# Last stage of a graph network on Trainium2: one-hots by ScalarE in place of VectorE

## The chip, the cores and the metric

The kernel runs on one core of a Trainium2 chip. The metric is the device time in microseconds, the median of several executions. Engines are called TensorE (PE; its weight loads are PEld), VectorE (DVE), ScalarE (ACT), GpSimd (POOL) and SyncE (SP, which here only starts DMAs). They run side by side and wait for each other on semaphores.

## What is computed

Two layers of a graph network on 3125 nodes of 512 features, with 50000 edges sorted by their target. The first layer is an attention over the edges, the second a mean over neighbours with two matrices. Cut to what matters, with `deg` the number of edges into a node, at least 1:

```python
h = maximum(layernorm(x), 0)
q, k = h @ Wq + bq, h @ Wk + bk                       # 8 heads
attn = softmax over the edges of a target of (q[rows] . k[cols])
x = x + segment_sum(attn * k[cols], rows) @ Wo + bo
h2 = maximum(layernorm(x), 0)
agg = segment_sum(h2[src], dst)                       # the last stage from here
x = x + h2 @ W1.T + b1 + (agg / deg) @ W2.T + b2
```

## The kernel before, in words

**Tiling.** The nodes are cut into NW = 25 windows of WIN = 125. The sorted edges are cut into chunks of 128 x CT = 128 x 17 edges, each belonging to one window, with padding; for these inputs the last stage has 25 chunks. `key` words hold the edge's source and target; chunk tables tell where each chunk begins, which window it belongs to and whether it continues one.

**Stages.** (1) layernorm, q and k, sorting of edges, up to about 400 us. (2) attention, chunk by chunk, to about 1205 us. (3) the Wo stage, about 1205 to 1323 us: for each window t, TensorE transposes the attention's rows (`wo_cols`) and multiplies by Wo (`wo`, L769 through `product`), VectorE adds the residual and takes statistics (`wo_sum`, `wo_stats`, `wo_norm`, L1396 to L1420), ScalarE takes the square root (L697) and makes h2 by a Relu (L700) in `h2`, and GpSimd's queue stores h2 to DRAM (`store_h2`, L540). ScalarE runs this by `ahead(act, NW, 2, h2_turned, h2)`: the copy of columns for window t+2 (`h2_turned`, with L567), then `h2` for window t. VectorE's L1412 of window t also waits until the store of window t-2 has landed. (4) the last stage, to the end.

**The last stage.** For chunk g, with b = g mod 2 for its buffers:
- GpSimd gathers 17 tiles of 128 rows of h2 by an indirect DMA each (L504), into `rows[:, b]`.
- VectorE in `agg(g)`: waits for TensorE's sum, adds it to `acc` (L1439), divides by the degree (L1445, `win_out`), then runs `next_hot`: it decodes chunk g+2 (L1216 to L1223: `idx` for the gathers and `loc`, the position of each edge's target in the window), makes the one-hots `oh` of chunk g+2 (`one_hot`, L1232) and sums them over the 17 tiles (`sum_hot`, L1387, for the degrees). Only after that it adds bias (L1456) and residual (L1459) to chunk g's product, which frees the store.
- TensorE in `agg(g)`: waits for `kept` (the sum of one-hots of chunk g), 34 matmuls one-hot x rows (L929), the product of the window's own h2 with W1 (L769), transposes of `win_out` and, when SyncE's load has landed, of the rows of h2 of chunk g+1 (`fin_cols`, L915), then the product with W2 (L769).
- ScalarE in `fin(g)`: two copies of transposed columns out of PSUM (`fin_turned`, L716), the second of them for the rows of chunk g+1. Nothing else in this stage.
- SyncE in `aggregate(g)`, in this order: the loads of indices and parameters of chunk g+2 (L367, L368), the load of h2 rows of chunk g+1 (`load_rows`, L449), the store of chunk g's output (`store_out`, L456); it waits until this store has landed before it goes on.

So the loads of the next round stand behind the store of this one on SyncE's queue, and the store stands behind VectorE's work for chunk g+2. Sets of one-hots 0 and 1 are made by VectorE after its Wo loop, before `agg(0)`:

```python
            for b in range(2):
                sum_hot(b, b)
```

`ag["oh_ready"]` counts finished sets of one-hots, `ag["acc_ready"]` finished sums of TensorE, `ag["decode"]` three steps for each decoded chunk. `within(g, count)` is true without a branch for g below 25.

Of the kernel before, what the change touches and what calls it, by code (L numbers as in the profile page):

```python
# [10 lines left out]
def build(nc, io):  # L11
# [5 lines left out]
    ALU, ACT, AX = mybir.AluOpType, mybir.ActivationFunctionType, mybir.AxisListType  # L17
# [5 lines left out]
    WIN = 125  # L23
    NW = N // WIN
# [3 lines left out]
    CT = 17  # L28
# [20 lines left out]
    with ctx:  # L49
        def sb(name, shape, dt=F32):  # L50
            return ctx.enter_context(nc.sbuf_tensor(name, shape, dt))
# [43 lines left out]
        oh = sb("oh", [128, 2, CT, WIN])  # L95
# [16 lines left out]
        oh_sum = junk[:, 0, 0:2 * WIN].rearrange("p (b n) -> p b n", b=2)  # L112
# [4 lines left out]
        bias = (acc, win_out)  # L117
# [28 lines left out]
        loc = sb("loc", [128, 2, CT + 2])  # L146
# [11 lines left out]
        ones = sb("ones", [128, 128])  # L158
        iota_i = arena[:, 4 * COLS:4 * COLS + 128].bitcast(I32)
        iota = sb("iota", [128, 128])  # L160
# [13 lines left out]
        whole_turn = turn[1][0:H, 0:256].rearrange("p (k n) -> p k n", k=2)  # L174
        alphap = turn[1][0:WIN, 256:256 + H]
        aggp = sums[0:WIN, 0:D]
        degp = tiny[0:WIN, 0:1]
        totp = tiny[:, 0:2 * NW].rearrange("p (j w) -> p j w", j=2)
        turned_keys = [sums[:, 0:COLS], sums[:, COLS:2 * COLS]]
# [2 lines left out]
        bias_parts = sem("bias_parts")  # L182
        XG = 5
        XT = NW // XG
        COUNTED = 20
        ROW_SPLIT = [(0, 112), (112, WIN)]
        x_in, w_in, bias_in, ends_in = [sem(f"x_in{n}") for n in range(XG)], sem("w_in"), sem("bias_in"), sem("ends_in")
# [35 lines left out]
        def chunk_sems(p):  # L223
            s = {n: sem(f"{p}_{n}") for n in ("pk_free", "idx_ready", "decode", "oh_ready", "step",
                                              "acc_free", "acc_ready", "out_ready", "out_free")}
            s["pk_in"] = [sem(f"{p}_pk_in{b}") for b in range(2)]
            s["rows_in"] = [[sem(f"{p}_rows_in{b}_{n}") for n in range(len(PARTS))] for b in range(2)]
            s["rows_free"] = [sem(f"{p}_rows_free{n}") for n in range(len(PARTS))]
            last = "store" if p == "at" else "kept"
            s[last] = sem(f"{p}_{last}")  # L230
            return s

        at, ag = chunk_sems("at"), chunk_sems("ag")
# [24 lines left out]
        def pairs(eng, n, body):  # L258

            for t in range(n):  # L260
                body(t, t % 2, t // 2)

        def ahead(eng, n, depth, first, body):

            for d in range(depth):
                first(d, d % 2, d // 2)

            def both(t, b, i):
                first(t + depth, (b + depth) % 2, i + (b + depth) // 2)
                body(t, b, i)  # L270
            pairs(eng, n - depth, both)
            for t in range(n - depth, n):
                body(t, t % 2, t // 2)

        def given(eng, condition, body):

            if condition is True:
                body()
            elif condition is not False:
                with eng.If(condition):  # L280
                    body()

        def within(g, count):
            return True if isinstance(g, int) and g < NW else g < count

        def rounds(eng, bound, pair):

            for i in range(SURE + 1):
                pair(i)
            with eng.If(bound > 2 * SURE + 2):  # L290
                with eng.Fori(0, GMAX // 2 - SURE - 1) as k:
                    pair(k + (SURE + 1))

        def chunks(eng, count, body):

            def pair(i):
                for b in range(2):
                    given(eng, within(i * 2 + b, count), lambda: body(i * 2 + b, b, i))
            rounds(eng, count, pair)
# [13 lines left out]
        def chunk_count(eng, j):  # L313
            return eng.value_load(chunk_i[0:1, j, 2, LAG:LAG + 1], min_val=NW, max_val=GMAX - 1)

        def chunk_count_after(eng, j):
            eng.wait_ge(sort_ready, j + 1)
            return chunk_count(eng, j)
# [5 lines left out]
        def _(sp):  # L324
# [5 lines left out]
            def load_x_group(n):  # L330
                tab = io["x"].rearrange("(t p) d -> p t d", p=WIN)[:, n * XT:(n + 1) * XT, :]
                for p0, p1 in ROW_SPLIT:
                    sp.dma_start(x_sb[p0:p1, n * XT:(n + 1) * XT, :], tab[p0:p1, :, :]).then_inc(x_in[n], 16)
            load_x_group(0)
# [218 lines left out]
        def _(act):  # L553
            def norm(n):

                group = rstd[:, n * XT:(n + 1) * XT]
                act.wait_ge(var_ready, n + 1)
                act.activation(group, group, ACT.Sqrt).then_inc(std_ready, 1)
                act.wait_ge(norm_ready, n + 1)
# [5 lines left out]
            def turned(t, b, i, s, ring, n=1):  # L565
                act.wait_ge(s["turn_ready"], t + 1)
                act.activation(ncol[:, b, :, :], turn[b][:, 0:KC * WIN].rearrange("p (c n) -> p c n", c=KC), ACT.Copy).then_inc(s["col_ready"], 1)  # L567
                act.wait_ge(s["col_ready"], t + 1)
                act.sem_inc(s["turn_free"], 1)
# [6 lines left out]
            def count_sides(k):  # L576

                for _ in range(k):
                    n = next(counts)
                    if n >= SIDES:  # L580
                        act.wait_ge(side_done, n - SIDES + 1)
                    act.activation(sides[:, n % SIDES, :], endf[:, n // NW, :], ACT.Sign, bias=edge[0:EP, n % NW:n % NW + 1],  # L582
                                   accum_out=cnt[:, n // NW, n % NW:n % NW + 1]).then_inc(side_done, 1)

            act.wait_ge(endf_ready, 1)
            count_sides(COUNTED)

# [20 lines left out]
            for t in range(NW):  # L608
                if (t + 4) % XT == 0 and t + 4 < NW:
                    norm((t + 4) // XT)  # L610
                if t + 1 < NW:
# [7 lines left out]
                act.activation(k_stage[t % STAGES], wide[t % 2][0:WIN, D:2 * D], ACT.Copy)  # L619
                if t < (2 * NW - COUNTED) // 3:  # L620
                    count_sides(3)
# [81 lines left out]
            def h2_turned(t, b, i):  # L703
# [1 line left out]
                act.activation(spare[:, :], ones[0:1, 0:1], ACT.Sqrt).then_inc(table_in, 1)  # L705
                act.wait_ge(table_in, t + 1)
                turned(t, b, i, s3, 2)
            ahead(act, NW, 2, h2_turned, h2)

            count1 = chunk_count_after(act, 1)  # L710

            def fin_turned(k, n, free):

                act.wait_ge(s5["turn_ready"], n)
                act.sem_inc(free, 1)
                act.activation(ncol[:, k, :, :], turn[k][:, 0:KC * WIN].rearrange("p (c n) -> p c n", c=KC), ACT.Copy).then_inc(s5["col_ready"], 1)  # L716
# [3 lines left out]
            def fin(g, b, i):  # L720
                fin_turned(1, g * 2 + 2, ag["out_free"])
                fin_turned(0, g * 2 + 3, s5["row_free"])
            chunks(act, count1, fin)


        @block.tensor
        def _(pe):
# [21 lines left out]
            def totals():  # L749
                pe.wait_ge(side_done, 2 * NW)  # L750
                pe.matmul(totp, ones[0:EP, :], cnt[:, :, :], start=True, stop=True).then_inc(tot_ready, 1)
# [32 lines left out]
            def leave(t, part, left):  # L784

                pe.wait_ge(part_ready[part], t + 1)
                pe.matmul(wide[t % 2][0:WIN, 0:D], minus[:, :], part_stage[t % STAGES][:, part, :], start=False, stop=True, skip_group_check=True).then_inc(left, 1)  # L787
# [3 lines left out]
            for t in range(NW):  # L791
# [13 lines left out]
                if t > 0:  # L805
                    leave(t - 1, 1, tail_left)
                if t == (2 * NW - COUNTED) // 3 + 1:
                    totals()
# [139 lines left out]
        def _(dve):  # L948
# [8 lines left out]
            def moments(n):  # L957

                dve.wait_ge(x_in[n], 16 * len(ROW_SPLIT))
                for t in range(n * XT, (n + 1) * XT):  # L960
                    dve.bn_stats(stats[:, t, :], x_sb[:, t, :]).then_inc(s1["step"], 1)
# [269 lines left out]
            def one_hot(s, g, b):  # L1231
                dve.tensor_tensor(oh[:, b, :, :], iota[:, 0:WIN].unsqueeze(1).to_broadcast([128, CT, WIN]),  # L1232
                                  loc[:, b, 1:CT + 1].unsqueeze(2).to_broadcast([128, CT, WIN]), ALU.is_equal).then_inc(s["oh_ready"], 1)
# [147 lines left out]
            count1 = chunk_count(dve, 1)  # L1381

            def sum_hot(g, b):

                one_hot(ag, g, b)
                dve.wait_ge(ag["oh_ready"], g + 1)
                dve.tensor_reduce(oh_sum[:, b, :], oh[:, b, :, :].rearrange("p t n -> p n t"), AX.X, ALU.add).then_inc(ag["kept"], 1)  # L1387
            for b in range(2):
                decode(ag, b, b, 0)

# [37 lines left out]
            for b in range(2):  # L1428
                sum_hot(b, b)
# [54 lines left out]
```

## Time and profile before

| | |
|---|---|
| median of 3 executions | 1931.77 us (1930.68 to 1932.28) |
| the profiled execution: time / span | 1932.3 us / 1930.5 us |
| TensorE matmuls / loads busy | 1666.8 us (86%) / 963.8 us (50%) |
| VectorE busy | 1336.3 us (69%) |
| ScalarE busy | 1001.1 us (52%) |
| GpSimd busy | 1141.1 us (59%) |
| gathers of the last stage, L504 | 425, mean 1049 ns |
| one-hots by VectorE, L1232 | 25, mean 2373 ns |
| their sums, L1387 | 25, mean 4165 ns |

Busy times are shares of the whole span, over stages with different limits. The span is what lies between the first and the last recorded instruction; the time of an execution has some us more around it. A row of a view names the line, the engine, the operation, output<-input, and in brackets the idle time before it with what ended it.

### The profile page before, as it was taken

How to read it: one execution, taken by the hardware profiler on the slowest of the kernel's cores; microseconds unless marked ns; L12 is line 12 of the kernel's file. 1: busy time of each engine (PE TensorE's matmuls, PEld its weight loads, DVE VectorE, ACT ScalarE, POOL GpSimd, SP SyncE). 2: the span in 40 equal slices, each digit the busy share in tenths (PEclk: the TensorE clock that was granted, in tenths of full speed). 3: DMA queues.
4: the chain of work that ended last, by engine and by line, in shares of the span. 5: the costliest groups of instructions: out<-in, count | busy, mean ns of one | idle time of the engine just before them, and what ended most of it. 6: DMA issues, size and time to landing. Idle time of an engine off the chain costs nothing.

```text
span 1930.5 us, 24219 instructions
## 1 busy us (share of the span) xinstructions
PE 1666.8 (86%) x5735; PEld 963.8 (50%) x5735; DVE 1336.3 (69%) x2587; ACT 1001.1 (52%) x3779; POOL 1141.1 (59%) x1323
## 2 busy tenths in 40 slices
PE   3799863688988889898888897895999999999998
PEld 1344331466666666666666666342444444444443
DVE  8768994888888989898988885465444444444441
ACT  4453313499999999999999997241000000000000
POOL 2000001878787878888787880013777777777773
PEclk9899876799999989999999999997999999999999
DMA  8122104665657565665657562945777777777774
GB/s 188 52 69 71 63 28 145 192 168 143 192 150 190 160 184 170 168 186 163 191 149 197 145 179 61 222 109 153 210 217 212 219 218 219 216 214 211 215 213 140
DMA packets 133201, 318.07 MB, mean 165 GB/s; under 512 B 41908, under 2 KB 42158, under 8 KB 133044
## 3 DMA queue, kind: packets, MB, share of 16 engines
q0 software_dynamic: 70240, 229.93, 41.8%
q1 hardware_dynamic: 62804, 86.44, 16.2%
q8 instruction: 50, 0.82, 0.2%
q14 instruction: 107, 0.88, 0.1%
HBM read 280.43 MB, written 35.86 MB: 164 GB/s over the span
## 4 chain that ended last, share of the span: by engine, by line
PE 51%; DVE 20%; issue 15%; POOL 7%; DMA 4%; ACT 2%; DVEq 1%; SPq 0%; POOLq 0%; ACTq 0%
PE wide L769 14%; PE sums L929 12%; PE sums L832 12%; PE wide L860 9%; POOL arena L504 7%; DVE nodes L1338 2%; DVE arena L1083 2%; DVE arena L1082 2%; DMA h2tab<-node 2%; DVE nodes L1284 1%; DVE nodes L1329 1%; DVE node L1225 1%; PE wide L782 1%; PE wide L787 1%; ACT arena L582 1%
## 5 line engine op out<-in xcount | busy, mean ns | idle before, releaser
L636 ACT ACTIVATE nodes<-arena,nodes 128x64 f32<-128x64 f32 x2840 | 682.7, 332 | 1.2 <-PE sums L832 1.2
L504 POOL DMA_INDIRECT arena<-ktab,idx x425 | 421.5, 992 | 188.1 <-issue 142.2
L504 POOL DMA_INDIRECT arena<-h2tab,idx x425 | 445.7, 1049 | 135.8 <-issue 134.9
L832 PE MATMUL sums<-nodes,oh 128*125 128x260 f32 x1768 | 466.7, 407 | 47.0 <-DVE nodes L1284 47.0
L769 PE MATMUL wide<-w_sb,node 128*125 128x512 f32 x1000 | 465.6, 610 | 20.7 <-ACT node L567 12.3
L832 PEld LDWEIGHTS sums<-nodes,oh 128*125 128x125 f32 x1768 | 342.0, 198 | 123.3 <-DVE nodes L1284 58.4
L929 PE MATMUL sums<-arena,oh 128*125 128x512 f32 x850 | 375.9, 600 | 6.9 <-DMA arena<-h2tab,idx 6.5
L716 ACT ACTIVATE node<-wide 128x500 f32<-128x500 f32 x51 | 27.3, 585 | 570.9 <-PE wide L915 570.8
L860 PE MATMUL wide<-q_win,node 125*128 125x512 bf16 x1275 | 310.3, 381 | 3.0 <-issue 3.0
L769 PEld LDWEIGHTS wide<-w_sb,node 128*125 128x125 f32 x1000 | 187.0, 193 | 230.8 <-issue 201.8
L1329 DVE TENSOR_TENSOR nodes<-wide,arena 128x1024 f32<-128x1024 f32 (+1 forms) x225 | 258.6, 1159 | 12.4 <-PE wide L860 11.8
L929 PEld LDWEIGHTS sums<-arena,oh 128*125 128x125 f32 x850 | 158.1, 189 | 204.7 <-issue 188.2
L1338 DVE TENSOR_REDUCE nodes<-nodes 128x16 f32<-128x1024 f32 (+1 forms) x225 | 256.9, 1151 | 0.0
L528 POOL TENSOR_SCALAR oh<-iota,loc 128x125 f32<-128x125 f32 x425 | 245.6, 592 | 0.8
L1439 DVE SCALAR_TENSOR_TENSOR acc<-acc,first_chunk,sums 125x512 f32<-125x512 f32 x25 | 18.7, 748 | 305.4 <-PE sums L929 305.4
L860 PEld LDWEIGHTS wide<-q_win,node 125*128 125x128 bf16 x1275 | 178.4, 141 | 91.9 <-issue 5.9
L510 POOL DMA_DIRECT2D sorted_tab<-arena x2 | 1.2, 612 | 287.8 <-DVE arena L1129 287.8
L1083 DVE TENSOR_TENSOR arena<-arena 128x256 f32<-128x256 f32 x272 | 113.9, 419 | 0.0
L1082 DVE TENSOR_TENSOR arena<-arena 128x256 f32<-128x256 f32 x272 | 113.6, 418 | 0.0
L1387 DVE TENSOR_REDUCE junk<-oh 128x125 f32<-128x2125 f32 x25 | 104.1, 4165 | 0.9
L540 POOL DMA_DIRECT2D h2tab<-node x25 | 13.4, 535 | 150.3 <-ACT node L700 144.4
L1232 DVE TENSOR_TENSOR oh<-iota,loc 128x2125 f32<-128x2125 f32 x25 | 59.3, 2373 | 4.0 <-DVE loc L1223 4.0
(202 smaller groups left out, 1165.9 us busy)
## 6 DMA issues: line engine op xcount, KB each, us to landing
node<-node_tab SPq DMA_DIRECT2D x27, 531.2 KB
q_win<-qtab SPq DMA_DIRECT2D x26, 336.0 KB
arena<-ktab,idx POOLq DMA_INDIRECT x425, 5.1
arena<-h2tab,idx POOLq DMA_INDIRECT x425, 3.9
h2tab<-node POOLq DMA_DIRECT2D x25, 250.0 KB, 2.7
node<-h2tab SPq DMA_DIRECT2D x26, 224.0 KB
qtab<-q_win SPq DMA_DIRECT2D x17, 336.0 KB
nodes<-x SPq DMA_DIRECT2D x5, 1120.0 KB
```

Of the source, the lines that this page charges most:

```text
L504: gp.indirect_dma_start(rows[:, b, t, :], None, tab, bass.IndirectOffsetOnAxis(ap=idx[:, b, t:t + 1], axis=0)).then_inc(s["rows_in"][b][PA ...
L528: last = gp.tensor_scalar(oh[:, b, t, :], iota[:, 0:WIN], loc[:, b, t + 1:t + 2], None, ALU.is_equal)
L636: last = act.activation(msgs[:, t, h // HH, h % HH * DH:(h % HH + 1) * DH], rows[:, 1 - b, t, h * DH:(h + 1) * DH], ACT.Copy, scale=den_in ...
L769: last = pe.matmul(out, ncol[:, b, c, :], w_sb[:, w, c, :], start=start and c == 0, stop=stop and c == KC - 1)
L832: last = pe.matmul(halves[:, u, :], oh[:, 1 - b, t, :], rhs[side][:, t, u, :], start=t == 0, stop=t == CT - 1)
L860: last = pe.matmul(wide[n % 2][:, (t - t0) * D:(t - t0 + 1) * D], ohT[:, b, :].rearrange("p (e t) -> p t e", t=CT)[:, t, :], q_win[:, b, p ...
L929: last = pe.matmul(aggp, oh[:, b, t, :], rows[:, b, t, :], start=t == 0, stop=t == CT - 1)
L1082: self.made(dve.tensor_tensor(new[:, :, 0, :], old[:, :, 0, :], old[:, :, 1, :], ALU.min))
L1083: self.made(dve.tensor_tensor(new[:, :, 1, :], old[:, :, 0, :], old[:, :, 1, :], ALU.max))
L1329: made.append(st.mark(dve.tensor_tensor(prod[:, n % 3, 0:k * D], wide[n % 2][:, 0:k * D], rows[:, b, t0:t0 + k, :].rearrange("p t d -> p ( ...
L1338: summed.append(st.mark(dve.tensor_reduce(sc[:, :, t0:t0 + k].rearrange("p h t -> p t h"), prod[:, (n - 1) % 3, 0:k * D].rearrange("p (t h ...
L1387: dve.tensor_reduce(oh_sum[:, b, :], oh[:, b, :, :].rearrange("p t n -> p n t"), AX.X, ALU.add).then_inc(ag["kept"], 1)
```

## The change

Each set of one-hots of the last stage is made by ScalarE in two steps: 17 activations, one for a tile, `(loc - iota)^2` for 125 columns, with `loc` as a per-partition bias; then one activation over all 2125 columns, `relu(1 - v)`, which gives 1 where the square was 0 and 0 elsewhere. Set g+2 is made in `fin(g)` behind the two copies. Sets 0 and 1 are made in the Wo stage, behind `h2` of windows 4 and 8. `oh_ready` counts two steps for a set. VectorE's `sum_hot` waits for the set and keeps the sum. `late_oh` is another name for `oh`.

```diff
+        late_oh = oh
+        HOT_AT = {4: 0, 8: 1}
@@ ScalarE
-            ahead(act, NW, 2, h2_turned, h2)
+            def late_hot(g, b, done=None):
+                act.wait_ge(ag["decode"], g * 3 + 3)
+                if done is not None:
+                    act.wait_ge(ag["acc_ready"], done)
+                for t in range(CT):
+                    last = act.activation(late_oh[:, b, t, :], iota[:, 0:WIN], ACT.Square, bias=loc[:, b, t + 1:t + 2], scale=-1.0)
+                last.then_inc(ag["oh_ready"], 1)
+                act.wait_ge(ag["oh_ready"], g * 2 + 1)
+                hot = late_oh[:, b, :, :].rearrange("p t n -> p (t n)")
+                act.activation(hot, hot, ACT.Relu, bias=ones[:, 0:1], scale=-1.0).then_inc(ag["oh_ready"], 1)
+
+            def h2_and_hot(t, b, i):
+                h2(t, b, i)
+                if t in HOT_AT:
+                    late_hot(HOT_AT[t], HOT_AT[t])
+            ahead(act, NW, 2, h2_turned, h2_and_hot)
@@ fin(g, b, i), ScalarE
                 fin_turned(1, g * 2 + 2, ag["out_free"])
                 fin_turned(0, g * 2 + 3, s5["row_free"])
+                given(act, within(g + 2, count1), lambda: late_hot(g + 2, b, g + 1))
@@ sum_hot(g, b), VectorE
-                one_hot(ag, g, b)
-                dve.wait_ge(ag["oh_ready"], g + 1)
-                dve.tensor_reduce(oh_sum[:, b, :], oh[:, b, :, :].rearrange("p t n -> p n t"), AX.X, ALU.add).then_inc(ag["kept"], 1)
+                dve.wait_ge(ag["oh_ready"], g * 2 + 2)
+                dve.tensor_reduce(oh_sum[:, b, :], late_oh[:, b, :, :].rearrange("p t n -> p n t"), AX.X, ALU.add).then_inc(ag["kept"], 1)
```

## Rows read from the trace of the kernel before

**Rows 1.** Busy time by stretch: us, busy and count per engine, PEclk, DMA share, GB/s.

```profile
1460.00:1900.00 440.00, 433.33 (x1139) 197.62 (x1138) 188.37 (x242) 20.35 (x38) 341.01 (x326) 1.00 0.74 216
```

**Rows 2.** Chain of waits, last stage: start us, us, what.

```profile
1583.34 4.68 DMA arena<-h2tab,idx
...
1615.75 3.43 PE wide L769 x8
...
1638.88 3.43 PE wide L769 x8
```

**Rows 3.** Timeline of one chunk: start us, us, engine, line; two SyncE rows are another chunk's.

```profile
1604.62 1.24 SPq L456 DMA_DIRECT2D out<-node  x2
1611.56 0.90 SPq L449 DMA_DIRECT2D node<-h2tab  x2
...
1619.01 2.37 DVE L1232 TENSOR_TENSOR oh<-iota,loc 128x2125 f32<-128x2125 f32 x1 [0.17 <-DVE loc L1223]
1619.34 0.46 PEld L915 LDWEIGHTS wide<-ident,node 125*128 125x128 f32 x4
1619.73 1.06 ACT L716 ACTIVATE node<-wide 128x500 f32<-128x500 f32 x2 [22.07 <-PE wide L915]
1621.41 4.16 DVE L1387 TENSOR_REDUCE junk<-oh 128x125 f32<-128x2125 f32 x1
1627.34 0.91 SPq L456 DMA_DIRECT2D out<-node  x2
1633.88 0.90 SPq L449 DMA_DIRECT2D node<-h2tab  x2
1642.48 0.46 PEld L915 LDWEIGHTS wide<-ident,node 125*128 125x128 f32 x4
```

**Rows 4.** GpSimd's timeline in the same chunk, and a row of the waits, 1325:1930.

```profile
1619.71 2.49 POOL L504 DMA_INDIRECT arena<-h2tab,idx  x1 [0.30 <-issue]
1622.50 0.95 POOL L504 DMA_INDIRECT arena<-h2tab,idx  x1 [0.30 <-issue]
...
PEld sums L929 <- DMA arena<-h2tab,idx: 16.3, 17, 4.3
```

**Rows 5.** Groups of ScalarE by shape: count, busy us, mean ns, idle before.

```profile
L636 ACT ACTIVATE nodes<-arena,nodes 128x64 f32<-128x64 f32 x2840 | 682.7, 332 | 1.2 <-PE sums L832 1.2
L582 ACT ACTIVATE arena<-junk,edge 125x400 bf16<-125x400 f32 x50 | 30.7, 619 | 9.9 <-DVEq L986 9.9
L700 ACT ACTIVATE node<-nodes,shift,rstd 125x512 f32<-125x512 f32 x25 | 20.3, 814 | 10.7 <-DVE shift L1420 10.7
L705 ACT ACT_TABLE_LOAD x1 | 1.3, 1283 | 0.7 <-issue 0.7
```

**Rows 6.** Timeline, start of last stage; median landing of gathers from the DMA view.

```profile
1330.29 0.90 SPq L449 DMA_DIRECT2D node<-h2tab  x2
1333.30 1.07 PE L915 MATMUL wide<-ident,node 125*128 125x125 f32 x4 [14.55 <-DMA node<-h2tab]
...
arena<-h2tab,idx POOLq DMA_INDIRECT x355, 4.0
```

**Rows 7.** Timeline of the Wo stage: ScalarE at windows 4, 5 and 8, VectorE at window 6.

```profile
1242.12 0.81 ACT L700 ACTIVATE node<-nodes,shift,rstd 125x512 f32<-125x512 f32 x1 [0.43 <-DVE shift L1420]
1245.92 0.20 ACT L697 ACTIVATE rstd<-rstd 125x1 f32<-125x1 f32 x1 [2.27 <-DVEq L1414]
...
1252.08 0.15 DVE L1412 TENSOR_SCALAR rstd<-mv 125x1 f32<-125x1 f32 x1 [2.96 <-POOLq L544]
...
1263.67 0.81 ACT L700 ACTIVATE node<-nodes,shift,rstd 125x512 f32<-125x512 f32 x1 [0.43 <-DVE shift L1420]
1264.61 0.59 ACT L567 ACTIVATE node<-wide 128x500 f32<-128x500 f32 x1
```

**Rows 8.** Chain of waits, Wo stage.

```profile
1265.25 3.70 PE wide L769 x8
1268.95 0.43 PE wide L764 x4
```

**Rows 9.** TensorE's timeline in the Wo stage, after a wait.

```profile
1233.05 5.37 PE L769 MATMUL wide<-w_sb,node 128*125 128x512 f32 x8 [3.17 <-ACT node L567]
```

## The prediction

> **What bounds the kernel now.** I read the page first for the stages, then the last stage by four views: busy time by stretch, the chain of waits, the timeline of one chunk, and the waits. From 1331 us to the end the kernel repeats one pattern 25 times, once for each chunk. In 440 us of it TensorE is busy for 433 at the full granted clock, ScalarE for 20, VectorE for 188 [rows 1]. The chain of waits gives the period: the products at L769 start at 1615.75 and again at 1638.88, so 23.13 us a chunk [rows 2]. TensorE waits for nobody inside it except some 0.3 us for ScalarE's copy. So the last stage is bound by TensorE, and work taken off VectorE buys nothing by itself. The chain did run through GpSimd's gathers up to 1583 us [rows 2], so GpSimd is the near second; yet TensorE's waits for gathers in the whole last stage are 16.3 us in 17 pieces, the longest 4.3 [rows 4].
>
> What is to be seen in the timeline of one chunk [rows 3] is a second loop that today has slack. P is the moment at which TensorE begins to transpose the next chunk's rows of h2 (PEld L915 node, 1619.34, next 1642.48). From P, ScalarE copies the columns (L716, over at 1620.79). VectorE has decoded chunk g+2 by then, compares (L1232, from 1619.01), sums the one-hots (L1387, from 1621.41), and only then adds the bias to chunk g's product and the residual (L1456, L1459). SyncE stores that at 1627.34 and, once the store has landed, issues the load of the next rows (L449) at 1633.88. Such a load took 3.0 us where TensorE waited for it (issued 1330.29, transposes from 1333.30 [rows 6]), so the rows are there at about 1637, some 5 us before TensorE wants them at 1642.48.
>
> **Removed.** One comparison of 128x2125 by VectorE per chunk, 2.37 us [rows 3]. While it runs, one gather's work on GpSimd lasts 2.49 us in place of 0.95 [rows 4]: 1.54 us of GpSimd per chunk. With 0.30 us between them, 16 plain gathers and this one make 16 x 1.25 + 2.79 = 22.8 us, under TensorE's 23.13, so I book the relief at nothing; its other bound is rival (b).
> The Trainium skill (SBUF — State Buffer, SBUF: two separate sides) says that a VectorE operation with two SBUF inputs and a GpSimd operation that reads SBUF shut each other out of a shared port for the whole instruction. The stretched row agrees with it. Taken as a reason for the change it would give 1.54 us a chunk wherever GpSimd is the bound, which is (b) below.
>
> **Added: the price on ScalarE.** The trace has no Square of 125 columns and no pass of 2125, so neighbours bound both. A 128x64 Copy with a per-partition scale lasts 332 ns, and 2840 of them are 682.7 us busy, so they follow each other at 0.240 us; a 400-column Sign with a per-partition bias lasts 619 ns [rows 5]. The slope between them is 287/336 = 0.85 ns a column. The 512-column Relu with both scale and bias from memory, 814 ns, gives 1.08 as upper end [rows 5]. A Square is then 0.240 + 61 x 0.00085 = 0.292 us after the one before and 0.384 us long, so 17 of them take 16 x 0.292 + 0.384 = 5.06 us (up to 5.3). The rectified pass takes 0.332 + 2061 x 0.00085 = 2.09 us (up to 2.55). With 0.1 us for the hand-overs, an estimate, a set of one-hots costs 7.25 us of ScalarE. I take the lower slope because these passes have one operand from memory, like the Sign. Square may want a table load of its own beside Sqrt: 0 or 1.28 us each way [rows 5]; I take 0 and keep the other end (5 us in all, in the Wo stage).
> The Trainium skill (ScalarE: Activation LUTs, Rules for kernel authors) advises VectorE and not ScalarE for relu, add and multiply. That speaks against this change, and the rows agree with 7.25 against 2.37 us; taken alone it says nothing of who waits, and ScalarE's idle time would make it worth 0 by [rows 1].
>
> **Where the 7.25 us lie in the last stage.** ScalarE is idle 22 of 23 us, so they fit its time. But they begin only behind its second copy, at P + 1.45, and VectorE now waits for them ahead of L1387, with the former chunk's L1456 and L1459 queued behind that wait, SyncE's store behind those, and SyncE's loads behind the store. The slack loop becomes, from P to the next P: copy 1.45 (1620.79 - 1619.34) + Squares 5.06 + rectified pass 2.09 + hand-overs 0.10 + from the start of the sum to the store's issue 5.93 (1621.41 to 1627.34) + from there to the issue of the row load 6.54 (1627.34 to 1633.88; the store's landing and two loads for chunk g+3) = 21.17 [rows 3, 5]. Then the rows must land. Bounds: 3.0 us [rows 6], and 4.0 us, the median of a gather of about the same size among all others [rows 6]. I take 3.3, nearer to the low end, because GpSimd, with 21.3 us of gathers in a longer period, will be idle about then. Sum: 24.47 us, 1.34 more than 23.13. TensorE waits that long at the transposes in each step that follows a set of one-hots. Sets are made for chunks 2 to 24, so in 23 steps; the last of these issues no load of indices ahead of its rows, which is worth about the 1.3 us, so 22 count: 22 x 1.34 = 29.5 us. Bounds: with landing 3.0 the loop is 24.17 and the stage pays 23 us; with landing 4.0, a store part of 6.94 (1604.62 to 1611.56, [rows 3]) and ScalarE's upper prices it is 26.3 and the stage pays 69, which wants all of them together.
> The delay holds the load of indices for the next decode too, but that is issued ahead of the rows, and today's decode is over at 1619.01, before P [rows 3], so it is not what comes last. The gathers hang on the decode as well; GpSimd runs half a chunk behind it, and that covers them.
>
> **Two sets in the stage before.** Sets 0 and 1 are now made by ScalarE behind windows 4 and 8 of the Wo stage. VectorE made them behind that stage, where TensorE stood 14.55 us waiting for the first rows of h2 [rows 6], hence at no cost: nothing is won at the end. ScalarE, though, is in the loop of each window. Behind window 4 (Relu over at 1242.93) its next statistics step moves from 1245.92 to 1242.93 + 7.25 + 0.8 for the copy between = 1251.0 [rows 7]. VectorE's pass takes about 3.3 us from there to L1412 of window 6, which comes at 1254.3 in place of 1252.08; it had stood there 2.96 us for a store [rows 7]. Some 2.1 us of delay stay, and I carry them to window 8; bounds 0 and 5, since the next stores are issued later too. Behind window 8 there is no cover: the copy at 1264.61 is what TensorE's products at 1265.25 wait for, and from there its products follow each other in the chain to the stage's end [rows 7, 8]. This set costs its full 7.25, with the carry 9.4 us. TensorE stands idle some 7 us before. A wait of 3.17 us at 1233.05 was followed by eight matmuls in 5.37 us against 3.70 [rows 8, 9], 1.67 lost; I add 2.0 (bounds 0 and 3.5). Stage: +11.4 us, bounds 7 and 16.
>
> **Sum.** 29.5 + 11.4 = +40.9 us on the profiled execution's 1932.3 us (span 1930.5 and 1.8 around it) = 1973.2. The profiled execution stood 0.5 us above the median of the runs, 1931.8, so the forecast is 1973 us.
>
> **Rivals.** (a) The loop stays below 23.13: it needs 1.34 us less than I count, for instance a landing and a store part shortened by a quieter DMA. Against: both store parts in the rows are over 6.5 us and the 3.0 us landing was a quiet one. Then only the Wo stage pays: 1932 + 11 = 1943 us.
> (b) Faster than before: GpSimd is the true bound of the last stage's first half, as the chain up to 1583 us has it [rows 2], and the comparison robs it of 1.54 us a chunk [rows 4]. Eleven chunks by 1.54 = 17 us off: 1915 us, if the new loop stays short and the Wo stage absorbs its sets. It decides only where TensorE's period is set by GpSimd's; against it stand GpSimd's own 22.8 us, and the 16.3 us of waits for gathers, 17 at most if all went.
> (c) ScalarE is dearer: the Squares don't overlap (0.384 apart, +1.5 us a set), or cost as the 814 ns row has it. 22 x 1.5 + 3 = 36 us more, 2009 us. Against it: 2840 passes in a row do overlap [rows 5].
> (d) The change does not bite: the sets are ready before VectorE asks for them and the windows' stores cover the rest. The queue allows it nowhere in the last stage. About 1932 us.
>
> **How the numbers follow.** Forecast 0.80; (a) 0.08; (b) 0.03; (c) 0.07; (d) 0.02. The range runs from 1950, half-way from the forecast's lower bound (23 + 7 us, 1962) to (a), to 1998, where landing is 4.0 us and the store part 6.94 (loop 25.57, +54 us, Wo stage 12). A measurement of this kernel can tell about 0.2% (4 us) from no change. Faster by more: (b), 0.03. Within: (d), 0.02. Slower: the rest, 0.95.
>
> **What would show it.** In the profile after: a period of the last stage of 24 to 25.6 us, and TensorE idle 1 to 2.4 us a chunk ahead of PE L915 node, put down to the DMA of the rows; ScalarE's set 7.0 to 7.6 us; VectorE's sum starting 8.7 us after P; no stretched gather on GpSimd, and idle time of its own; in the Wo stage the products of 1265.25 some 9 us later, and slow at first. I am wrong if the period stays 23.1, if TensorE waits for gathers or for the sum of one-hots instead, or if the Wo stage grows by less than 7 us.

## The result, and the profile after

The changed kernel takes 1994.01 us, the median of 4 runs (1990.80 to 1996.57), against 1932.03 us (1930.68 to 1933.87) for the kernel before: a ratio of 1.0319 [1.0301, 1.0337]. The forecast was 1973 us with a range of 1950 to 1998. The profiled execution took 1990.8 us, with a span of 1989.0. It is set against the former one's 1932.3.

The difference lies in two stages. I measured each between two marks that both kernels have. From the first transposes of `win_out` to the last (24 periods) the last stage went from 1363.20 to 1919.75, 556.55 us, and now goes from 1370.51 to 1978.26, 607.75 us: +51.2. Before, all periods lay between 23.13 and 23.55 us; now they range from 23.13 to 29.81 with a mean of 25.3. From the first Relu of the Wo stage to the last it was 1220.30 to 1322.44, 102.14 us, and is 1215.97 to 1330.15, 114.18 us: +12.0. The attention part, which the change doesn't touch, ended 4.3 us earlier in this execution. 1932.3 - 4.3 + 12.0 + 51.2 = 1991.2, against 1990.8.

First the page after, section 1 and two groups of section 5 (busy us, mean ns, idle before).

```profile
PE 1674.7 (84%) x5735; PEld 964.5 (48%) x5735; DVE 1276.5 (64%) x2562; ACT 1177.8 (59%) x4229; POOL 1101.6 (55%) x1323
...
L506 POOL DMA_INDIRECT arena<-h2tab,idx x425 | 405.7, 955 | 211.9 <-issue 129.2
...
L1405 DVE TENSOR_REDUCE junk<-oh 128x125 f32<-128x2125 f32 x25 | 104.1, 4167 | 219.7 <-ACT oh L720 219.7
```

VectorE and GpSimd have less to do (60 us and 40 us less), and the gathers' mean fell from 1049 to 955 ns, so the change does relieve both. What to read is the last number of the last line: VectorE now stands 219.7 us in front of its sums, waiting for ScalarE.

The stretch that answers [rows 1] (us; busy and count of PE, PEld, DVE, ACT, POOL; PEclk; DMA share; GB/s), and rows of the waits of the last stage (sum, count, longest).

```profile
1380.00:1980.00 600.00, 554.18 (x1422) 252.68 (x1421) 178.80 (x279) 181.39 (x444) 374.39 (x392) 0.97 0.68 193
...
DVE junk L1405 <- ACT oh L720: 219.7, 23, 11.2
POOL arena L506 <- DVE idx L1235: 82.7, 22, 5.9
PE wide L934 <- DMA node<-h2tab: 59.5, 22, 14.7
```

TensorE was busy 98% of such a stretch and is now busy 92%. It waits for the rows of h2, 59.5 us in all, of which 14.7 are the old wait ahead of the stage. That leaves 44.8 us in 21 steps, 2.1 each. GpSimd, the former near second, idles 82.7 us.

The chain of waits in the last stage, which answers [rows 2] (start, us, what):

```profile
1652.64 0.66 PE wide L934 x4
1653.89 5.03 ACT oh L716 x17
1658.94 2.08 ACT oh L720
...
1667.50 3.82 DMA out<-node
...
1674.61 4.26 DMA node<-h2tab
1678.91 1.09 PE wide L934 x4
```

The chain names the new loop: transposes, ScalarE's set, VectorE, store, load, transposes. From 1652.64 to 1678.91 it took 26.27 us. TensorE's products, which were the chain in [rows 2], are out of it. The timeline of the same chunk, to be laid beside [rows 3]:

```profile
1652.64 0.65 PE L934 MATMUL wide<-ident,node 125*128 125x125 f32 x4 [1.89 <-DMA node<-h2tab]
...
1653.89 5.02 ACT L716 ACTIVATE oh<-iota,loc 128x125 f32<-128x125 f32 x17
1658.94 2.07 ACT L720 ACTIVATE oh<-oh,ones 128x2125 f32<-128x2125 f32 x1
1661.04 4.17 DVE L1405 TENSOR_REDUCE junk<-oh 128x125 f32<-128x2125 f32 x1 [9.58 <-ACT oh L720]
...
1666.97 0.91 SPq L458 DMA_DIRECT2D out<-node  x2
...
1674.07 0.90 SPq L451 DMA_DIRECT2D node<-h2tab  x2
...
1678.91 1.09 PE L934 MATMUL wide<-ident,node 125*128 125x125 f32 x4 [3.52 <-DMA node<-h2tab]
1679.80 4.80 PE L788 MATMUL wide<-w_sb,node 128*125 128x512 f32 x8
```

The loop is 8.40 us to the sum (1652.64 to 1661.04), 5.93 to the store, 7.10 to the row load and 4.84 until TensorE has the rows. Over the stage, with steps that have all of these, the store part has a mean of 6.90 us (22 steps) and the landing one of 4.20 (21 steps, 2.90 to 5.18).

In the Wo stage ScalarE's timeline answers [rows 7]:

```profile
1238.57 5.01 ACT L716 ACTIVATE oh<-iota,loc 128x125 f32<-128x125 f32 x17
1243.61 2.07 ACT L720 ACTIVATE oh<-oh,ones 128x2125 f32<-128x2125 f32 x1
1246.51 0.20 ACT L699 ACTIVATE rstd<-rstd 125x1 f32<-125x1 f32 x1
...
1262.07 5.01 ACT L716 ACTIVATE oh<-iota,loc 128x125 f32<-128x125 f32 x17
1267.12 2.07 ACT L720 ACTIVATE oh<-oh,ones 128x2125 f32<-128x2125 f32 x1
1269.31 0.59 ACT L569 ACTIVATE node<-wide 128x500 f32<-128x500 f32 x1
```

and TensorE behind that last copy answers [rows 8]:

```profile
1269.94 6.70 PE L788 MATMUL wide<-w_sb,node 128*125 128x512 f32 x8 [4.97 <-ACT node L569]
```

From its Relu at 1220.30 the kernel before needed 43.37 us to the Relu of window 8. It is now 45.38: a carry of 2.0. Then the set costs its full length, and the product behind it lasts 6.70 us in place of 3.70.

### The profile page after: what moved, and what is told of

It reads as the page before. It is cut to its first block, busy times and chain, and to the rows that moved or that the text cites. A ratio compares the mean times of both kernels' runs of the same rounds, so it can differ in the third digit from the quotient of the medians.

```text
span 1989.0 us, 24669 instructions
## 1 busy us (share of the span) xinstructions
PE 1674.7 (84%) x5735; PEld 964.5 (48%) x5735; DVE 1276.5 (64%) x2562; ACT 1177.8 (59%) x4229; POOL 1101.6 (55%) x1323
## 4 chain that ended last, share of the span: by engine, by line
PE 35%; DVE 22%; issue 17%; DMA 11%; ACT 10%; SPq 3%; DVEq 1%; POOL 1%; POOLq 0%; ACTq 0%
PE wide L788 10%; PE sums L851 10%; PE wide L879 8%; ACT oh L716 6%; DMA node<-h2tab 4%; DMA out<-node 4%; PE sums L948 2%; DVE nodes L1357 2%; ACT oh L720 2%; DVE arena L1102 2%; DVE arena L1101 2%; DMA h2tab<-node 2%; DVE nodes L1303 1%; DVE node L1244 1%; DVE nodes L1348 1%
## 5 line engine op out<-in xcount | busy, mean ns | idle before, releaser
L506 POOL DMA_INDIRECT arena<-h2tab,idx x425 | 405.7, 955 | 211.9 <-issue 129.2
L788 PE MATMUL wide<-w_sb,node 128*125 128x512 f32 x1000 | 481.9, 627 | 21.0 <-ACT node L569 19.6
L851 PE MATMUL sums<-nodes,oh 128*125 128x260 f32 x1768 | 456.2, 400 | 47.3 <-DVE nodes L1303 47.3
L851 PEld LDWEIGHTS sums<-nodes,oh 128*125 128x125 f32 x1768 | 335.4, 194 | 121.2 <-DVE nodes L1303 58.7
L788 PEld LDWEIGHTS wide<-w_sb,node 128*125 128x125 f32 x1000 | 194.0, 200 | 237.3 <-issue 213.5
L734 ACT ACTIVATE node<-wide 128x500 f32<-128x500 f32 x51 | 29.5, 587 | 458.3 <-PE wide L934 458.3
L1405 DVE TENSOR_REDUCE junk<-oh 128x125 f32<-128x2125 f32 x25 | 104.1, 4167 | 219.7 <-ACT oh L720 219.7
L716 ACT ACTIVATE oh<-iota,loc 128x125 f32<-128x125 f32 x425 | 125.5, 388 | 0.0
L1102 DVE TENSOR_TENSOR arena<-arena 128x256 f32<-128x256 f32 x272 | 116.9, 430 | 0.0
L1101 DVE TENSOR_TENSOR arena<-arena 128x256 f32<-128x256 f32 x272 | 116.6, 429 | 0.0
```

The lines of the kernel that those rows point to most:

```text
L506: gp.indirect_dma_start(rows[:, b, t, :], None, tab, bass.IndirectOffsetOnAxis(ap=idx[:, b, t:t + 1], axis=0)).then_inc(s["rows_in"][b][PA ...
L716: last = act.activation(late_oh[:, b, t, :], iota[:, 0:WIN], ACT.Square, bias=loc[:, b, t + 1:t + 2], scale=-1.0)
L788: last = pe.matmul(out, ncol[:, b, c, :], w_sb[:, w, c, :], start=start and c == 0, stop=stop and c == KC - 1)
L851: last = pe.matmul(halves[:, u, :], oh[:, 1 - b, t, :], rhs[side][:, t, u, :], start=t == 0, stop=t == CT - 1)
L1101: self.made(dve.tensor_tensor(new[:, :, 0, :], old[:, :, 0, :], old[:, :, 1, :], ALU.min))
L1102: self.made(dve.tensor_tensor(new[:, :, 1, :], old[:, :, 0, :], old[:, :, 1, :], ALU.max))
```

## The experiments

The theory: VectorE's wait for ScalarE holds back chunk g's output, and with it store and row load, so this loop, some 25.5 us long, sets the period; two sets in the Wo stage add their own delay. Two repairs follow that leave the sets on ScalarE: VectorE finishes the output before it waits for the set (output first), or SyncE loads the rows ahead of the store (rows ahead). The rivals were that ScalarE's price itself, or a transfer under contention, sets the period wherever the work stands.

The twelve runs fell under two conditions. Along with the eight labelled e1 to e7 and f8 the kernel before took 2213 to 2238 us, along with f3, f4, f6 and f7 it took 1933 to 1934 us, nearly as in the result above. I call the first the long condition. Some of the expectations put it down to the chip, but chip number 7 of the record stands for both, 1934 us with f4 and 2238 us with f8; what makes the difference is not known. What tells the theories apart is read from the four runs at 1933 to 1934 us, and the others are told behind them.

**f4: output first.** Applied to the changed kernel, VectorE decodes chunk g+2 where it did, and sums its one-hots behind L1477, which frees the store:

```diff
-                def next_hot():
-                    decode(ag, g + 2, b, i + 1)
-                    sum_hot(g + 2, b)
-                given(dve, within(g + 2, count1), next_hot)
+                given(dve, within(g + 2, count1), lambda: decode(ag, g + 2, b, i + 1))
@@ behind L1477, the addition of the residual
+                given(dve, within(g + 2, count1), lambda: sum_hot(g + 2, b))
```

> The kernel of e4_output_first again, on another chip (the chips of the e runs took 2213 to 2238 us for the kernel before in place of 1932, with other waits than those of the case's profiles). On a chip that takes 1932 us for the kernel before, theory A gives 1943 us (loop cut, period 23.13, only the Wo stage pays), theory B 1994 us. On a slow chip: 0.985 of the kernel before, as measured.

Measured: 1939.94 us, ratio 1.0033 [1.0021, 1.0046]. The 24 periods take 555.48 us, 1.1 less than before the change; the Wo stage keeps its 112.56. In TensorE's timeline two transposes of `win_out` follow each other after 23.14 us, and VectorE's waits for ScalarE in the stage fell from 219.7 to 44.5 us:

```profile
1395.15 0.59 PE L934 MATMUL wide<-ident,win_out 125*128 125x125 f32 x4
...
1418.29 0.59 PE L934 MATMUL wide<-ident,win_out 125*128 125x125 f32 x4
...
DVE junk L1405 <- ACT oh L720: 44.5, 22, 2.0
```

The loss of the last stage is gone although ScalarE does the same work at the same place. So the loss came from what stood behind VectorE's wait; ScalarE's price alone does not cause it.

**f7: both repairs.** f4, and sets 0 and 1 made by VectorE behind its Wo loop, as before:

```diff
-        HOT_AT = {4: 0, 8: 1}
+        HOT_AT = {}
@@ VectorE, behind the Wo loop
-                sum_hot(b, b)
+                sum_hot(b, b, True)
@@ sum_hot(g, b, by_dve=False)
+                if by_dve:
+                    one_hot(ag, g, b)
+                    dve.wait_ge(ag["oh_ready"], g * 2 + 1)
+                    dve.sem_inc(ag["oh_ready"], 1)
```

> The kernel of e7_before_but_act again: sets 0 and 1 by VectorE behind the Wo stage, sets 2 to 24 by ScalarE, output added before VectorE waits for a set. If the chip takes about 1932 us for the kernel before: the difference to f4 (1940) is what the two sets in the Wo stage cost. By my forecast 11.4 us: 1929 to 1932 us. If f4's 6 us over the kernel before are all of their cost: 1933 us.

Measured: 1930.13 us (1928.46 to 1933.99), ratio 0.9984 [0.9974, 0.9993]. Wo stage 102.48 us, 24 periods 555.47. Against f4 it is 9.8 us faster: the price of the two sets in the Wo stage. The other repair, f4's, is worth 54 us (1994.0 to 1939.9). In this kernel's timeline the store is out before VectorE turns to the sum:

```profile
1643.78 0.69 DVE L1475 TENSOR_TENSOR node<-wide,junk 125x512 f32<-125x512 f32 x1 [5.36 <-PE wide L788]
...
1645.64 0.91 SPq L458 DMA_DIRECT2D out<-node  x2
1647.44 4.17 DVE L1409 TENSOR_REDUCE junk<-oh 128x125 f32<-128x2125 f32 x1 [2.02 <-ACT oh L720]
```

With ScalarE's sets and no cost of their own, this kernel is 3 us (0.16%) ahead of the kernel before. The interval leaves out 1, but only just, and 0.2% was what the prediction took a measurement to be able to tell. So much, or so little, is the change worth once its two costs are mended.

**f3: rows ahead.** VectorE's order as in the changed kernel; SyncE loads rows two chunks ahead, and issues that load before the store:

```diff
+            load_rows(1, 1)
...
-                load_rows(g + 1, 1 - b)
+                given(sp, within(g + 1, count1), lambda: load_rows(g + 2, b))
```

> The kernel of e3_rows_ahead again (rows of h2 loaded two chunks ahead, before the store; all else as in the changed kernel). If the chip takes about 1932 us for the kernel before: theory A 1940 us, as f4 did, since TensorE waits no more for rows; should the rest of the loop (store, load of indices, decode, set, sum) be longer than 23.13, up to 1955. Theory B, the store of the output itself or VectorE's wait is the cost and not the rows: 1984 us or more.

Measured: 1953.6 us, ratio 1.0102 [1.0081, 1.0122]; the 24 periods take 569.95 us, 37.8 less than in the changed kernel, so the row load held most of the loss, but not all. The first periods are 23.13, later ones up to 25.34. The timeline of one of these, and a row of the waits:

```profile
1650.38 0.91 SPq L458 DMA_DIRECT2D out<-node  x2
...
1662.02 0.18 DVE L1236 TENSOR_SCALAR idx<-pk 128x17 int32<-128x17 int32 x1 [9.73 <-DMA par<-chunk_tab]
...
1675.73 0.91 SPq L458 DMA_DIRECT2D out<-node  x2
1677.83 0.65 PE L935 MATMUL wide<-ident,win_out 125*128 125x125 f32 x4 [1.99 <-DVEq L1465]
...
PEld wide L935 <- DVEq L1465: 21.2, 15, 2.8
```

VectorE waits 9.73 us for the parameters of chunk g+2, whose load stands behind the store too. From store to store it is 25.35 us by way of that load, the decode, the set and the sum. My prediction had dismissed it ("not what comes last"). That was right while the rows came later; with the rows out of the way it is the next loop.

**f6: four Squares fewer.** Sets 2 to 24 leave out tiles 0 to 3, so they are 1.18 us shorter:

```diff
-                for t in range(CT):
+                for t in ((range(4, CT)) if done is not None else range(CT)):
```

> The kernel of e6_four_less again: 13 Squares in place of 17 in each set of the last stage; tiles 0 to 3 keep what their buffer held, so the sums of the second layer are not the reference's. If the chip takes about 1932 us for the kernel before: 1.17 us less in the loop, theory A 22 x 1.17 = 26 us less, 1968 us; with TensorE's slow stretches after long waits gone as well, 1960 us or less. Theory B (ScalarE's idle time hides the set) 1990 us or more.

Measured: 1977.02 us, ratio 1.0226 [1.0206, 1.0246]; periods 590.12 us in sum, 17.6 less than with all Squares, where 22 x 1.18 = 26 us would go if nothing else in the loop moved. That lies between the two theories' times, so both missed the size; but the time did fall by 17 us, so the set does stand in the loop. What was lost is in the landing, whose mean rose from 4.20 to 4.60 us. One step, with GpSimd's gather beside the row load:

```profile
1663.96 0.95 POOL L506 DMA_INDIRECT arena<-h2tab,idx  x1 [0.30 <-issue]
1664.40 0.90 SPq L451 DMA_DIRECT2D node<-h2tab  x2
...
1669.43 0.65 PE L934 MATMUL wide<-ident,node 125*128 125x125 f32 x4 [1.24 <-DMA node<-h2tab]
```

The load is issued while a gather runs, and takes 5.03 us. Of the 22 steps in which TensorE waited for it, 17 had the load issued during the gathers or up to 0.22 us behind them, and it took 4.21 to 5.55 us; in the other 5 it was issued 0.45 to 0.67 us behind and took 3.43 to 3.98.

**The long condition.** The same edits, and their inverse, where the kernel before takes 2213 to 2238 us. e1 gives sets 2 to 24 back to VectorE (`True` makes `sum_hot` compare first, as in f7) and leaves only 0 and 1 with ScalarE:

```diff
-                given(act, within(g + 2, count1), lambda: late_hot(g + 2, b, g + 1))
@@ next_hot, VectorE
-                    sum_hot(g + 2, b)
+                    sum_hot(g + 2, b, True)
```

> The changed kernel with the sets of the last stage (2 to 24) made by VectorE again; ScalarE makes only sets 0 and 1, behind windows 4 and 8 of the Wo stage. Theory A (the queue loop: ScalarE's set, sum, store, load of rows, transposes): the last stage has its 23.13 us period again and only the Wo stage pays, some 11.5 us: 1943 us. Theory B (a set of ScalarE costs its share wherever it is made, by what it disturbs: 62 us / 25 = 2.5 us each): 1937 us.

Measured: 2232.93 us, ratio 1.000 [0.997, 1.0029].

e2 gives back sets 0 and 1 alone (`HOT_AT = {}`, as in f7):

> The changed kernel with sets 0 and 1 made by VectorE behind the Wo stage, as before; ScalarE makes sets 2 to 24. Theory A: the Wo stage gives back its 11.5 us, the last stage keeps its loop: 1982 us. Theory B: two sets of 25 less: 1989 us. A third reading, that set 0 behind window 4 is wholly covered by the stores and set 1 costs only its bare 7.1 us, gives 1987.

Measured: 2196.94 us, ratio 0.9816 [0.9752, 0.988].

e3 is the edit of f3, e4 that of f4, e7 that of f7:

> The changed kernel, but SyncE loads the rows of h2 two chunks ahead, ahead of the store instead of behind it; all else unchanged, ScalarE still makes all sets. Theory A: TensorE waits no more for rows; what is left of the loop (store, load of indices, decode, set, sum, store) is about 23.4 us and has half a chunk of slack to eat: last stage 51 us shorter, 1943 us. Theory B: the rows are not the cause, at most some 10 us are won: 1984 us or more.

> The changed kernel, but VectorE adds bias and residual of chunk g (and so frees its store) before it waits for set g+2 and sums it. ScalarE's passes are the same and at the same place. Theory A: the loop is cut, period 23.13: 1943 us. Theory B: 1994 us, nothing changes.

> Both repairs at once: sets 0 and 1 by VectorE behind the Wo stage, sets 2 to 24 by ScalarE, and VectorE adds the output before it waits for a set. Theory A: both costs are gone and TensorE's 23.13 us are left: 1932 us, the same as before within 3 us. VectorE's comparison is off GpSimd's back here (21.3 us of gathers a chunk in place of 22.8), so if GpSimd had been the bound of the stage's first half, this would be some 17 us faster, 1915 us.

Measured: e3 2197.78, ratio 0.9839 [0.9774, 0.9904]; e4 2205.4, 0.9872 [0.9802, 0.9943]; e7 2186.01, 0.9868 [0.9788, 0.9948]. The expectations were reckoned from 1932 us for the kernel before, and this condition fits neither theory's picture: kernels that should have been equal to the kernel before or slower are 1.3 to 1.8% faster (e2, e3, e4, e7), and e1 equals it. These are misses, and the changed kernel itself was not run under this condition.

e5 adds four Squares to each set of the last stage, e6 is the edit of f6:

```diff
+                if done is not None:
+                    for k in range(4):
+                        act.activation(junk[:, 0, 256 + 128 * k:256 + 128 * k + WIN], iota[:, 0:WIN], ACT.Square, bias=loc[:, b, k + 1:k + 2], scale=-1.0)
```

> The changed kernel with four more Squares of 125 columns ahead of each set of the last stage, written to an unused place. Each is 0.292 us, 1.17 us a set. Theory A, the loop goes through ScalarE's set: 22 times 1.17 = +26 us, 2020 us. Theory B, ScalarE has 15 us of idle time a chunk that hides them: 1994 to 1998 us.

> The changed kernel with 13 Squares in place of 17 in each set of the last stage; tiles 0 to 3 keep what their buffer held, so the sums of the second layer are not the reference's. 1.17 us less a set. Theory A: -26 us, 1968 us. Theory B: 1990 to 1994 us. If the excess of the loop over my forecast came from TensorE's slow stretches after long waits, the gain is above 26 us, since the waits get short enough to end them: 1960 us or less.

Measured: e5 2202.97 us, ratio 0.9961 [0.992, 1.0001]; e6 2183.0, 0.9848 [0.9786, 0.9909]. Both are misses too. Between them, eight Squares, 2.36 us a set, are worth 20 us here, 0.9 a step.

Part of the difference lies in the last stage. (Part lies ahead of it: its first transposes of `win_out` come at about 1500 to 1530 us, in place of 1361 to 1372.) The median of its periods is 29.25 us in e1, 28.1 to 28.2 in e2 and e5, and 27.6 to 27.75 in e3, e4, e6 and e7, where the changed kernel and f3 to f7 had means of 23.1 to 25.3. TensorE and VectorE in e1:

```profile
1941.02 3.60 PE L787 MATMUL wide<-w_sb,node 128*125 128x512 f32 x8
...
1946.96 0.75 DVE L1460 SCALAR_TENSOR_TENSOR acc<-acc,first_chunk,sums 125x512 f32<-125x512 f32 x1 [17.55 <-remote]
```

VectorE's first step of a chunk comes 5.9 us after TensorE has finished the sum and gone on to its product (the means of the seven e runs are 3.3 to 4.7; in the changed kernel it comes after 0.2), released by something that the profile cannot name ("remote"). f8 asks whether the gathers do it. It leaves out tiles 13 to 16 of each chunk's gathers in the last stage, so its sums use old rows there and are not the reference's:

```diff
+                    if s is ag and t >= 13:
+                        continue
...
-                    pe.wait_ge(ag["rows_in"][b][n], (i + 1) * k * 16)
+                    pe.wait_ge(ag["rows_in"][b][n], (i + 1) * (1 if n == len(PARTS) - 1 else k) * 16)
```

> The changed kernel, but in the last stage GpSimd gathers only tiles 0 to 12 of each chunk; TensorE still multiplies all 17, the last four with what lies in the buffer, so the sums of the second layer are not the reference's. The gathers then end 5 us earlier, before the load of the rows is issued. In the changed kernel the rows land 4.20 us after issue in the mean of 21 steps, and the store part is 6.90. If the tail of the gathers holds the rows back (theory A'), landing falls to about 3.0 and the store part to about 6.5: 22 x 1.6 = 35 us less, about 1959 us where the kernel before takes 1932. If 4.2 us is the load's own time (theory B'), nothing of the loop moves: 1990 to 1994 us.

Measured: 2125.98 us, ratio 0.9507 [0.9458, 0.9555], a mean period of 24.6 us. The times expected were for the other condition, so the time itself decides nothing. The same two rows:

```profile
1917.90 3.60 PE L790 MATMUL wide<-w_sb,node 128*125 128x512 f32 x8
1918.11 0.75 DVE L1459 SCALAR_TENSOR_TENSOR acc<-acc,first_chunk,sums 125x512 f32<-125x512 f32 x1 [5.99 <-PE sums L950]
```

VectorE follows at 0.21 us and the store part, with means of 10.2, 9.0 and 10.6 us in e2, e5 and e6, has one of 6.97, about the changed kernel's 6.90 and not the 6.5 of theory A'. With four gathers in 17 gone both symptoms are gone. That ties them to the gathers; whether to their traffic or to their instructions, and by what way they delay VectorE's start, is left open.

On the question that the expectation put, f8 speaks for theory A': the row load, issued 4.5 us or more behind the last gather of the set, landed in 3.03 us in the mean (17 steps in which TensorE waited for it, 2.70 to 3.77). e2 says the same with all its gathers: its load comes 3.4 to 5.3 us behind the last of them and landed in 2.93 (20 steps). So what holds the load up is gone a few us behind the gathers.

## Why the prediction was right, point by point

**What bounds the kernel** held. The slack loop of [rows 3] became the period, TensorE waits at the transposes for the DMA of the rows, and GpSimd idles. f4 and f7 show it: take the output out from behind the wait, and the loss of the last stage is 0. The size came out short: +62 us against a forecast of +41, and 1994 us lies just inside the upper end of the range, 1998.

**ScalarE's price** was right to 2%. The groups by shape, after:

```profile
L716 ACT ACTIVATE oh<-iota,loc 128x125 f32<-128x125 f32 x425 | 125.5, 388 | 0.0
L720 ACT ACTIVATE oh<-oh,ones 128x2125 f32<-128x2125 f32 x25 | 51.7, 2067 | 0.8
```

Squares of 388 ns start 0.295 us apart (forecast 384 and 0.292), the rectified pass lasts 2.07 us (forecast 2.09), a set 7.12 us (forecast 7.25), and no table load was added for Square (four single ones in either profile). The slope between two shapes of [rows 5] was enough for a shape that the trace did not have; the reason that I gave for the lower slope was not tested.
The Trainium skill (ScalarE: Activation LUTs, What ACT_TABLE_LOAD costs) gives 280 ns and 0.833 ns a column for an activation with such a bias. An estimate by them is 384 ns for the Square and 2050 for the pass, and the 388 and 2067 ns here agree to about 1%.

**The loop** was sized too short: 24.47 us forecast, 25.5 measured as the sum of the means. From P to the start of the sum it took 8.46 (8.70 forecast; the copy and its hand-over were 1.25 in most steps and not 1.45), from there to the store 5.95 (5.93). The store part was 6.90 where I took 6.54, one row of [rows 3] with a second one at 6.94 beside it. The main miss is the landing, 4.20 where I took 3.3 "because GpSimd ... will be idle about then". In 9 of the 21 steps GpSimd still ran a gather when the load was issued, so that reason failed there. In the step shown above it was idle, but the transfers of its last gathers were not over:

```profile
1671.94 0.94 POOL L506 DMA_INDIRECT arena<-h2tab,idx  x1 [0.30 <-issue]
...
1677.40 0.94 POOL L506 DMA_INDIRECT arena<-h2tab,idx  x1 [4.52 <-DVE idx L1235]
```

The last gather of the set is issued by 1672.88. The 1 us stretches behind it (columns as in the stretch above; PEclk, DMA share and GB/s are the last three; the last two rows are for the clock, read further below):

```profile
1674.00:1675.00 1.00, 1.00 (x5) 0.47 (x4) 0.00 (x0) 0.00 (x0) 0.00 (x0) 1.00 0.71 218
1675.00:1676.00 1.00, 0.39 (x4) 0.16 (x2) 0.00 (x0) 0.49 (x1) 0.00 (x0) 1.00 0.87 186
1676.00:1677.00 1.00, 0.00 (x0) 0.00 (x0) 0.54 (x4) 0.10 (x1) 0.00 (x0) 1.00 0.28 96
1677.00:1678.00 1.00, 0.00 (x0) 0.00 (x0) 0.00 (x0) 0.00 (x0) 0.59 (x1) 1.00 0.06 10
1678.00:1679.00 1.00, 0.09 (x1) 0.09 (x2) 0.00 (x0) 0.00 (x0) 0.70 (x2) 0.90 0.02 6
1679.00:1680.00 1.00, 1.00 (x5) 1.00 (x6) 0.00 (x0) 0.00 (x0) 0.70 (x2) 0.50 0.73 201
```

From 1674 to 1678 the DMA engines moved 510 KB. The row load issued at 1674.07 is 250 KB of it, so about as much again belonged to transfers begun before, one gather's worth (128 rows of 2 KB). This is an estimate. Over 19 steps, a load issued less than 1.2 us after the end of the last gather's instruction landed in 4.17 to 5.18 us (12 steps, in most of which it still ran), and one issued 1.35 us or more behind it in 2.90 to 3.58 (7 steps). f6, e2 and f8 above have the same order, though not a sharp border, and single loads far behind the gathers took up to 4.24 us (e5, e6). Both ends of my bounds, 3.0 and 4.0, were thus real cases, and the first of them was the quiet one that I had called so. Landing and store part together are 1.26 us a step over the forecast, the part before them 0.22 under it. 22 steps by 1.04 make 23 us, and the stage shows 21.7 (51.2 against 29.5). So this was the right loop with a term of it, the landing, and to a lesser part the store part, sized too small.

**The Wo stage**: +12.0 us against a forecast of 11.4, and 9.8 by the difference of f4 and f7. The carry was 2.0 (2.1), the set 7.1 (7.25) and the slow product 3.0 (2.0).

**The rivals.** (a), a loop below 23.13, fell: transfers got longer, not shorter. (b), the gain by GpSimd's relief, fell in size. Five periods of the kernel before, 1479 to 1596, lasted 23.20 to 23.54 us, with waits for gathers in them, and these are gone in f4 and f7, but it is 1.1 us in all. GpSimd's 22.8 us were worked out with a stretched gather of 2.49 us; in many chunks it took 3.06, which makes 23.4, over the period. By the mean of 1049 ns it is 17 x 1.35 = 22.9 us, just under it. (c) fell: 0.295 us apart, not 0.388. (d) fell: VectorE stands 219.7 us.

## What to carry to other kernels

Before an operation goes to an idle engine, look at what is queued behind the consumer's wait: here 7.1 us of work on an engine that idles 22 of 23 us cost 2.1 us of TensorE's time a chunk, because a store and then a load stood behind VectorE's wait, and it cost nothing once VectorE finished the output first. Write out the slack loop, with every DMA in it, and add to it before comparing it with the bound. And size a transfer in it by what else the DMA engines move when it is issued, not by whether the issuing engine of the other transfers is idle.

## What the runs showed of the hardware

- In the changed kernel a row load of 2 DMAs landed in 2.9 to 3.6 us when issued 1.35 us or more behind the last gather's instruction, and in 4.2 to 5.2 when issued earlier. So moving a load earlier gives back less than it moves: 17.6 of 26 us in f6.
- TensorE's clock fell around some of the waits for rows and not around others. At the wait of 3.52 us the granted clock is 1.00 of 2.4 GHz up to 1678, 0.90 in the next stretch and 0.50, the level of 1.2 GHz, in the one from 1679, and the product at 1679.80 took 4.80 us in place of 3.60. Nine products of the last stage took 4.66 to 5.59 us, behind waits of 1.93 to 4.67 us. But behind four other waits, of 2.35, 2.73, 3.08 and 3.11 us, the product took 3.60 and the clock stayed at 1.00 around the one of 3.08, so the length of the wait alone does not tell. Three steps, 24.20 to 24.99 us long, had a slow product and no wait for rows at all. The stage's mean granted clock was 0.97, before it was 1.00 [rows 1].
- Without the comparison the gathers' instructions are 955 ns each, with it 1049. The Trainium skill (SBUF — State Buffer, SBUF: two separate sides) describes the shared port by which a VectorE operation with two SBUF inputs holds up GpSimd. The traces agree: the longest gather of the last stage took 3.07 us with that operation in the kernel and 1.45 without it.
- The same kernel took 1932 us under one condition and 2213 to 2238 under another, on the chip numbered 7 both 1934 and 2238, and the ranking of variants changed with it. With VectorE's order left as the change has it, a last stage with ScalarE's sets had the shorter period under the long condition (28.2 us in e2, 29.25 in e1 with VectorE's) and the longer one here (25.3 against 23.2). Nobody should rank two variants from runs of different conditions.
